# A step of its own for the layer norm's factor in the projection stage of a windowed-attention layer

## The chip, the core and the metric

The kernel runs on one core of one Trainium2 chip. The metric is the device time of one execution in microseconds (us), the median of several runs. The engines are TensorE (PE in the profile, PEld for its weight loads), VectorE (DVE), ScalarE (ACT), GpSimd (POOL) and SyncE (SP), which issues the transfers.

## The reference, cut to what matters

One transformer layer on x of shape 4 x 2048 x 256: x + attention(norm(x)), then a feed-forward part with ternary weights on the norm of that. The change lies in the first norm, ahead of the projections:

```python
def _layernorm(x, axis=-1, eps=1e-05):
    m = jnp.mean(x, axis=axis, keepdims=True)
    v = jnp.var(x, axis=axis, keepdims=True)
    return (x - m) / jnp.sqrt(v + eps)
...
        q = (x @ Wq.T).reshape(Bb, Tt, H, HD).transpose(0, 2, 1, 3)
        k = (x @ Wk.T).reshape(Bb, Tt, H, HD).transpose(0, 2, 1, 3)
        v = (x @ Wv.T).reshape(Bb, Tt, H, HD).transpose(0, 2, 1, 3)
```

Here x is already the normed one. Attention has 16 heads of 16, a window of 128 keys on either side, and key 0 visible to all. All is float32.

## The kernel before, in words

The kernel has a projection stage (`stage_project`, about 0 to 218 us), then one block with attention and the feed-forward part. Only the projection stage is touched in substance.

**Tiling.** The 8192 rows of x are 16 groups g of 512 rows, each group 4 blocks (t) of 128 rows. A group passes through a software pipeline of steps. In step i an engine works on different groups at once: `at(lag)` is group i - lag. Before the change the lags are LN = 1 (statistics and factor), LT = 2 (turning, that is transposing the normed rows), LP = 3 (projection). x itself is loaded by SP in step i = g (L337).

**The norm of a group.** VectorE: four `bn_stats` (L137), four `bn_aggr` that give mean and variance (L145), variance + eps (L148). ScalarE: the square root (L152). VectorE again, in `rstd`: reciprocal r0 (L158) and one Newton step in four small operations, t = (v+eps)*r0 (L160), t = t*r0 (L162), t = 1.5 - 0.5t (L164), rstd = t*r0 (L166); then `shifts`, shift = -mean*rstd (L195). All of these work on tiles of 128x4, and each waits for the one before it. In the next step ScalarE writes xn = x*rstd + shift, one 128x256 block at a time (L201, `scale_act`), TensorE turns the eight 128x128 pieces into two PSUM banks (L444, `turn()`), ScalarE copies them out as xt_hi (L569) and VectorE subtracts to get xt_lo (L673).

**The projection of a group q.** TensorE makes four banks u = 0 to 3 (two of Q, two of K) with `three_pass` (L221 to L223, 6 matmuls of 512 columns for each bank), with `turn()` of the next group between u = 2 and u = 3, then four blocks of V (24 matmuls of 272 columns). For each u: ScalarE copies the high bf16 part (`high`, L537), VectorE the rest (`rest_of`, L651 for Q, L655 for K), ScalarE the middle part (`mid`, L542), GpSimd the low part (L394, a 128x512 subtraction of two SBUF tiles), and for K a small fill of a gap column (L405, at the start of a sequence also L403). ScalarE copies V out (`v`, L547). SP stores the parts (L345, L351), V (L353), and then loads the next x (L337); SP does all of this in the order of the code.

**The order inside a step is written out by hand for each engine.** ScalarE before: xn 0 and 1, high(0), xn 2, high(1), xn 3, high(2), xt_hi twice, mid(0), high(3), v(0), mid(1), v(1), root, mid(2), v(2), mid(3), v(3). VectorE before: rest(0), stats 0 and 1, rest(1), stats 2, rest(2), xt_lo twice, stats 3, rest(3), `spread` (aggregate and eps), `rstd`, `shifts`, then the weights' parts (`dve_part`: sums of absolute values L910, and in eleven of the steps, two more operations each on 128x256, L931 and L933).

**The start.** Steps 0 to 2 are run by hand among the preparations: VectorE handles group 0, then the x0 row, `w_low(0)`, the statistics of group 1, q0, step LT, `w_low(1)`, wv_lo, and then the steps from LP on. GpSimd copies wv_hi for the other sequences there (L384).

`weights`, `Group`, `wait`, `step` are as in the listing; `wait` is a semaphore wait that is left out for a value of zero.

## Time and profile before

| | us |
|---|---|
| median of 3 runs | 1227.88 |
| lowest and highest run | 1227.07, 1853.66 |
| the profiled execution, its own time | 1227.89 |
| its span in the profile | 1226.1 |
| PE busy | 1156.5 |
| DVE busy | 1017.4 |
| ACT busy | 826.1 |
| POOL busy | 696.1 |

The profiled execution's own time is 1.8 us over its span, and equals the median. In the timeline rows below the columns are start (us), duration (us), engine, line, operation, written tile <- read tiles, shapes and count; in brackets stands the idle time of the engine before it and what ended that. Successive operations of one engine overlap a little in their records, so the distance from start to start is what an operation costs in a row of them. The projection stage's steady steps lie between 30 and 185 us. The granted clock of TensorE was full there (1.00).

### The profile page before, as it was taken

What the parts mean: (1) busy time and instruction counts of PE and PEld (TensorE: products, weight loads), DVE (VectorE), ACT (ScalarE), POOL (GpSimd) and SP (SyncE); (2) the same over time, 40 slices, a digit from 0 to 9 for tenths busy, and PEclk for the clock granted to TensorE, in tenths of its full rate; (3) what the DMA queues carried; (4) which work ended last, traced back from release to release, by engine and by line L of the source; (5) the groups of instructions that cost most, each with busy time, mean ns of one, the idle gap of its engine ahead of it and who ended that gap; (6) DMA issues with size and microseconds to landing.
All of it is one profiled execution on the core that took longest, in us unless ns stands there. A gap on an engine that the chain in (4) does not pass through costs nothing.

```text
span 1226.1 us, 26405 instructions
## 1 busy us (share of the span) xinstructions
PE 1156.5 (94%) x9051; PEld 762.1 (62%) x9051; DVE 1017.4 (83%) x3202; ACT 826.1 (67%) x1381; POOL 696.1 (57%) x930
## 2 busy tenths in 40 slices
PE   6888888599999999999999999999999999999997
PEld 5777775144444444444444444445889889889886
DVE  6889984788888888888888888886788888888885
ACT  5777774067777877777777777776665565565564
POOL 4445443457777777777777777676443343343344
PEclk8999998589999999999999999999999999999999
DMA  4797863854345643565435654314031221221200
GB/s 142 236 285 240 253 215 132 153 131 108 103 113 131 150 118 89 123 153 120 122 103 125 146 131 106 102 39 155 20 102 53 71 85 52 71 85 53 70 18 35
DMA packets 141253, 145.23 MB, mean 118 GB/s; under 512 B 23084, under 2 KB 134720, under 8 KB 141120
## 3 DMA queue, kind: packets, MB, share of 16 engines
q1 hardware_dynamic: 141120, 143.55, 44.0%
q8 instruction: 72, 1.18, 0.4%
q14 instruction: 61, 0.50, 0.2%
HBM read 91.74 MB, written 50.95 MB: 116 GB/s over the span
## 4 chain that ended last, share of the span: by engine, by line
PE 64%; DVE 7%; SPq 5%; issue 2%; DMA 1%; POOL 1%; ACT 1%; DVEq 0%; POOLq 0%
PE e_psum L1361 14%; PE e_psum L1403 13%; PE e_psum L1381 12%; PE e_psum L1671 5%; PE e_psum L1673 5%; SPq L1191 4%; PE e_psum L1651 3%; PE e_psum L1652 3%; PE e_psum L1099 2%; DVE n_stats L137 2%; DVE f_x L1770 2%; DMA e_q<-a_shift 1%; PE e_psum L1656 1%; PE e_psum L1620 1%; PE e_psum L223 1%
## 5 line engine op out<-in xcount | busy, mean ns | idle before, releaser
L1499 DVE CUSTOM_DVE_ANT_0 a_masked<-e_psum,a_band 128x387 f32<-128x387 f32 (+1 forms) x1024 | 502.7, 536 | 74.3 <-PE e_psum L1361 68.3
L1455 ACT ACTIVATE a_weights<-e_psum 128x1024 f32<-128x1024 f32 x384 | 385.8, 1022 | 111.2 <-PE e_psum L1381 111.1
L1361 PE MATMUL e_psum<-e_k,e_q 96*128 96x387 bf16 (+1 forms) x1024 | 328.0, 332 | 15.2 <-DMA e_q<-q_parts 11.2
L1260 POOL TENSOR_SCALAR_AFFINE_SELECT a_weights<-a_weights 128x1024 f32<-128x1024 f32 x256 | 275.7, 1090 | 51.4 <-ACT a_weights L1455 51.4
L1381 PE MATMUL e_psum<-e_q,e_k 128*128 128x384 bf16 (+2 forms) x1408 | 271.6, 278 | 6.9 <-DMA e_q<-a_shift 5.9
L1712 POOL TENSOR_TENSOR f_square<-f_relu 128x512 f32<-128x512 f32 x128 | 144.3, 1128 | 210.6 <-ACT f_relu L1701 198.9
L1361 PEld LDWEIGHTS e_psum<-e_k,e_q 96*128 96x128 bf16 x1024 | 93.8, 97 | 203.6 <-DVE a_max L1499 104.2
L1403 PE MATMUL e_psum<-a_weights,a_v 128*17 128x384 f32 (+2 forms) x2816 | 208.0, 393 | 1.3 <-POOL a_weights L1260 1.1
L1381 PEld LDWEIGHTS e_psum<-e_q,e_k 128*128 128x128 bf16 x1408 | 136.8, 99 | 65.1 <-DMA e_q<-a_shift 7.6
L1671 PE MATMUL e_psum<-w_w_t,f_square_hi 128*128 128x256 f32 x512 | 129.0, 287 | 5.5 <-DVE f_square_lo L1758 5.5
L1673 PE MATMUL e_psum<-w_w_t,f_square_lo 128*128 128x256 f32 x512 | 125.9, 281 | 0.0
L1701 ACT ACTIVATE f_relu<-e_psum,w_mag 128x512 f32<-128x512 f32 x128 | 87.5, 684 | 52.5 <-PE e_psum L1656 52.5
L1758 DVE TENSOR_TENSOR f_square_lo<-f_square,f_square_hi 128x512 fp32r<-128x512 f32 x128 | 98.6, 791 | 24.1 <-POOL f_square L1712 24.1
L1671 PEld LDWEIGHTS e_psum<-w_w_t,f_square_hi 128*128 128x128 f32 x512 | 96.2, 188 | 15.2 <-DVE f_square_lo L1758 12.0
L1651 PE MATMUL e_psum<-f_xt_hi,w_w_t 128*128 128x512 f32 x256 | 102.8, 402 | 1.1 <-ACT f_relu L1701 1.1
L1652 PE MATMUL e_psum<-f_xt_lo,w_w_t 128*128 128x512 f32 x256 | 101.2, 395 | 0.0
L1673 PEld LDWEIGHTS e_psum<-w_w_t,f_square_lo 128*128 128x128 f32 x512 | 96.5, 188 | 2.9
L1403 PEld LDWEIGHTS e_psum<-a_weights,a_v 128*17 128x17 f32 x2816 | 55.2, 96 | 65.6 <-issue 61.3
L394 POOL TENSOR_TENSOR p_q_parts<-p_rest,p_q_parts 128x512 bf16<-128x512 f32 x32 | 38.0, 1188 | 88.3 <-ACT p_q_parts L542 88.3
L1268 POOL TENSOR_TENSOR a_shift<-a_neg_rest,a_shift 16x128 bf16<-16x128 f32 x64 | 26.7, 417 | 107.4 <-ACT a_shift L1461 107.4
L1704 ACT ACTIVATE f_square_hi<-f_relu 128x512 fp32r<-128x512 f32 x128 | 81.0, 633 | 4.1
L1499 DVE DVE_READ_ACCUMULATOR2_ANT a_max<- 128x1 f32 x1024 | 83.6, 82 | 0.0
(207 smaller groups left out, 2046.3 us busy)
## 6 DMA issues: line engine op xcount, KB each, us to landing
k_parts<-p_k_parts SPq DMA_DIRECT2D x96, 129.0 KB, 2.8
e_k<-k_parts SPq DMA_DIRECT2D x64, 193.5 KB, 3.8
e_k<-k_parts SPq DMA_DIRECT2D x192, 64.5 KB, 3.3
q_parts<-p_q_parts SPq DMA_DIRECT2D x96, 128.0 KB, 3.0
e_q<-q_parts SPq DMA_DIRECT2D x64, 192.0 KB, 3.5
e_q<-q_parts SPq DMA_DIRECT2D x192, 64.0 KB, 3.2
v_ones<-p_va SPq DMA_DIRECT2D x16, 544.0 KB, 3.7
p_x<-in_x SPq DMA_DIRECT2D x16, 512.0 KB, 5.6
```

Source lines behind the costliest of these rows:

```text
L1260: pool.affine_select(out=blocks, in_=blocks, compare_op=ALU.is_ge, fill=0.0, base=0, pattern=[[0, NQ // 2 * HEAD_COLS // P // CUT_STEP], [ ...
L1361: pe.matmul(turn[TURN_OF_TILE[j] % TURN_BANKS][:, lo:hi], qw[ux.q][0:SLOT_ROWS, h, t * P:t * P + P], kt[ux.hq][0:SLOT_ROWS, h, start + lo: ...
L1381: ins = pe.matmul(score[c % 2][:, (n % 2) * GT + col * P:(n % 2) * GT + (col + m) * P], kt[us.hq][:, h, k0:k0 + P], qw[us.q][:, h, qb * P: ...
L1403: ins = pe.matmul(sum_bank[32 * j:32 * j + VW, qb * P:(qb + m) * P], vw[:, up.gpar, kb + 1, h * VW:h * VW + VW], pe_w[:, up.upar, c0:c0 + ...
L1455: act.activation(pe_w[:, us.upar, c * CHUNK:(c + 1) * CHUNK], score[c % 2][:], ACT.Exp).then_inc(s_exp, 1)
L1499: dve.tensor_tensor_reduce(out=masked[:, ux.upar, h, t:t + hi - lo], in0=bank[:, lo:hi], in1=band[:, lo:hi], scale=1.0, scalar=NEG, op0=AL ...
L1651: pe.matmul(self.h_bank[j % 2][:], lhs, self.sh.xt_hi[:, q.par, k, :], start=(k == 0), stop=False)
L1652: pe.matmul(self.h_bank[j % 2][:], lhs, self.sh.xt_lo[:, q.par, k, :], start=False, stop=False)
L1671: pe.matmul(y, sh.r2_hi[:, j % 4, part], self.w.w2_t[:, j, :], start=(j == 0 and t == 0), stop=False, skip_group_check=True)
L1673: ins = pe.matmul(y, sh.r2_lo[:, j % 4, part], self.w.w2_t[:, j, :], start=False, stop=(j == MH - 1), skip_group_check=True)
L1712: pool.tensor_tensor(sh.r2[:, j % 4, :], sh.r[:, j % 4, :], sh.r[:, j % 4, :], ALU.mult).then_inc(self.s_sq, 1)
L1758: dve.tensor_tensor(sh.r2_lo[:, j % 4, :], sh.r2[:, j % 4, :], sh.r2_hi[:, j % 4, :].bitcast(F32), ALU.subtract).then_inc(self.s_r2lo, 1)
```

## The change

The norm's factor (root, reciprocal, Newton step, shift) leaves the step of the statistics and gets a lag of its own, LF = 2; turning moves to LT = 3 and projection to LP = 4. ScalarE's root now adds eps itself through its bias, reads the variance tile, and stands between high(0) and xn 2 in place of between v(1) and mid(2). VectorE's separate eps addition goes; the Newton step is two `scalar_tensor_tensor` after the first product in place of three operations: t = (v + eps)*r0, t = (-0.5 t)*r0, rstd = (t + 1.5)*r0. The reciprocal and the first product stand after rest(0) and stats 0, the others after rest(1). The statistics are spread otherwise: block 0 after rest(0), block 1 after xt_lo, blocks 2 and 3 with the aggregate after rest(3). The statistics of group 2 are taken by hand before the first projection step. Cut to its core:

```diff
+        self.eps = sb("eps", [P, 1])
...
     def blocks(self, v, x, q, blocks):
+        if 0 in blocks:
+            wait(v, self.s_step, q.g * 3)
...
+    def aggregate(self, v, q):
+        v.wait_ge(self.s_step, q.g * 3 + 1)
+        for t in range(TB):
+            ins = v.bn_aggr(self.mv[:, q.par, t, :], self.stats[:, t, :])
+        ins.then_inc(self.s_step, 2)
+
+    def root_eps(self, a, q):
+        a.wait_ge(self.s_step, q.g * 3 + 3)
+        a.activation(self.sd[:, q.par, :], self.mv[:, q.par, :, 1], ACT.Sqrt, bias=self.eps[:, 0:1]
+                     ).then_inc(self.s_sd, 1)
+
+    def factor_begin(self, v, q):
+        base = q.g * 3
+        v.wait_ge(self.s_sd, q.g + 1)
+        v.reciprocal(self.r0[:], self.sd[:, q.par, :]).then_inc(self.s_back, 1)
+        v.wait_ge(self.s_back, base + 1)
+        v.scalar_tensor_tensor(out=self.t0[:], in0=self.mv[:, q.par, :, 1], scalar=EPS, in1=self.r0[:],
+                               op0=ALU.add, op1=ALU.mult).then_inc(self.s_back, 1)
+
+    def factor_end(self, v, q):
+        base = q.g * 3
+        v.wait_ge(self.s_back, base + 2)
+        v.scalar_tensor_tensor(out=self.t0[:], in0=self.t0[:], scalar=-0.5, in1=self.r0[:],
+                               op0=ALU.mult, op1=ALU.mult).then_inc(self.s_back, 1)
+        v.wait_ge(self.s_back, base + 3)
+        v.scalar_tensor_tensor(out=self.rs[:, q.par], in0=self.t0[:], scalar=1.5, in1=self.r0[:],
+                               op0=ALU.add, op1=ALU.mult).then_inc(self.s_shift, 1)
+        v.wait_ge(self.s_shift, q.g * 2 + 1)
         v.scalar_tensor_tensor(out=self.shift[:, q.par], in0=self.mv[:, q.par, :, 0], scalar=-1.0,
                                in1=self.rs[:, q.par], op0=ALU.mult, op1=ALU.mult).then_inc(self.s_shift, 1)
...
-        LN, LT, LP = 1, 2, 3
+        LN, LF, LT, LP = 1, 2, 3, 4
...
                     high(0)
+                if f:
+                    norm.root_eps(act, f)
                 if t:
                     norm.scale_act(act, xb[:, t.ring], xn[:, t.par], t, (2,))
...
                     v(1)
-                if n:
-                    norm.root(act, n)
-                if q:
                     mid(2)
...
-                first = n if n and n.g != 1 else None
+                first = n if n and n.g not in (1, 2) else None
...
                     rest_of(0)
                 if first:
                     dve.wait_ge(s_x[n.ring], (n.turn + 1) * DMA)
-                    norm.blocks(dve, xb[:, n.ring], n, (0, 1))
+                    norm.blocks(dve, xb[:, n.ring], n, (0,))
+                if f:
+                    norm.factor_begin(dve, f)
                 if q:
                     rest_of(1)
-                if first:
-                    norm.blocks(dve, xb[:, n.ring], n, (2,))
+                if f:
+                    norm.factor_end(dve, f)
                 if q:
                     rest_of(2)
...
                 if first:
-                    norm.blocks(dve, xb[:, n.ring], n, (3,))
+                    norm.blocks(dve, xb[:, n.ring], n, (1,))
                 if q:
                     rest_of(3)
                 if first:
-                    norm.spread(dve, n)
-                if n:
-                    norm.rstd(dve, n)
-                    norm.shifts(dve, n)
+                    norm.blocks(dve, xb[:, n.ring], n, (2, 3))
+                    norm.aggregate(dve, n)
...
             dve.wait_ge(s_x[1], DMA)
-            norm.front(dve, xb[:, 1], Group(1))
+            norm.blocks(dve, xb[:, 1], Group(1), range(TB))
+            norm.aggregate(dve, Group(1))
...
                               wv_hi[:, :, :, D:D + H].bitcast(F32), ALU.subtract).then_inc(s_clo, 1)
+            dve.wait_ge(s_x[2], DMA)
+            norm.blocks(dve, xb[:, 2], Group(2), range(TB))
+            norm.aggregate(dve, Group(2))
             for i in range(LP, G + LP):
```

The feed-forward part's norm still uses `front`, `root` and `rstd`; it gets the one added wait of `blocks`.

## Rows read from the trace of the kernel before

**Rows 1.** Busy time of each engine in two projection steps; columns named in the first line.

```profile
core 0: us, PE busy (x) PEld busy (x) DVE busy (x) ACT busy (x) POOL busy (x), PEclk, DMA share, GB/s
...
85.50:96.80 11.30, 9.74 (x58) 8.33 (x57) 9.81 (x24) 8.63 (x20) 4.97 (x7) 1.00 0.93 292
96.80:108.10 11.30, 9.74 (x58) 8.31 (x57) 10.76 (x25) 8.63 (x20) 4.97 (x7) 1.00 0.77 247
```

**Rows 2.** Waits of 40 to 180 us: us in total, times, longest us.

```profile
ACT p_xn L201 <- DVE n_shift L195: 23.4, 13, 2.0
```

**Rows 3.** Timeline of PE, one step.

```profile
102.44 1.09 PE L444 MATMUL p_bank<-p_ident,p_xn 128*128 128x128 f32 x8 [1.56 <-ACT p_xn L201]
...
107.84 0.40 PE L221 MATMUL p_bank<-p_xt_hi,p_wt_hi 128*128 128x512 f32 x1
...
111.80 0.40 PE L223 MATMUL p_bank<-p_xt_hi,p_wt_lo 128*128 128x512 f32 x1
```

**Rows 4.** Timeline of ACT, the end of one step and the start of the next.

```profile
108.24 0.39 ACT L547 ACTIVATE p_va<-p_bank 128x272 f32<-128x272 f32 x1
110.67 1.09 ACT L201 ACTIVATE p_xn<-p_x,n_shift,n_rstd 128x256 f32<-128x256 f32 x2 [2.04 <-DVE n_shift L195]
```

**Rows 5.** Timeline of DVE, the norm's factor in one step.

```profile
106.61 0.17 DVE L148 TENSOR_SCALAR n_var_eps<-n_meanvar 128x4 f32<-128x4 f32 x1
107.05 0.18 DVE L158 RECIPROCAL n_rstd_first<-n_stddev 128x4 f32<-128x4 f32 x1 [0.27 <-ACT n_stddev L152]
107.26 0.65 DVE L160 TENSOR_TENSOR n_newton<-n_var_eps,n_rstd_first 128x4 f32<-128x4 f32 x1
107.94 1.05 DVE L162 TENSOR_TENSOR n_newton<-n_newton,n_rstd_first 128x4 f32<-128x4 f32 x1
...
109.23 1.14 DVE L166 TENSOR_TENSOR n_rstd<-n_newton,n_rstd_first 128x4 f32<-128x4 f32 x1
110.41 0.16 DVE L195 SCALAR_TENSOR_TENSOR n_shift<-n_meanvar,n_rstd 128x4 f32<-128x4 f32 x1
110.49 0.43 DVE L931 TENSOR_TENSOR z_below<-z_w_in,z_nhalf 128x256 f32<-128x256 f32 x1
```

**Rows 6.** Timeline of POOL at the same time.

```profile
107.84 1.13 POOL L394 TENSOR_TENSOR p_k_parts<-p_rest,p_k_parts 128x512 bf16<-128x512 f32 x1
...
109.23 1.13 POOL L394 TENSOR_TENSOR p_k_parts<-p_rest,p_k_parts 128x512 bf16<-128x512 f32 x1
110.44 0.25 POOL L405 TENSOR_TENSOR p_k_parts<-p_key,p_one 128x12 bf16<-128x12 bf16 x1
```

**Rows 7.** Timeline of ACT, then of PE: turns of the first, second and last step.

```profile
24.55 0.59 ACT L201 ACTIVATE p_xn<-p_x,n_shift,n_rstd 128x256 f32<-128x256 f32 x1
...
25.26 1.03 PE L444 MATMUL p_bank<-p_ident,p_xn 128*128 128x128 f32 x8
...
35.60 1.09 PE L444 MATMUL p_bank<-p_ident,p_xn 128*128 128x128 f32 x8 [0.58 <-ACT p_xn L201]
...
179.67 1.09 PE L444 MATMUL p_bank<-p_ident,p_xn 128*128 128x128 f32 x8 [1.56 <-ACT p_xn L201]
```

**Rows 8.** Timeline of ACT, DVE and PE before the first projection step.

```profile
13.21 2.08 ACT L201 ACTIVATE p_xn<-p_x,n_shift,n_rstd 128x256 f32<-128x256 f32 x4 [2.05 <-DVE n_shift L195]
...
15.63 0.38 DVE L145 BATCH_NORM_AGGREGATE n_meanvar<-n_stats 128x2 f32<-128x6 f32 x4
...
15.34 1.97 PE L444 MATMUL p_bank<-p_ident,p_xn 128*128 128x128 f32 x8 [0.25 <-ACT p_xn L201]
```

**Rows 9.** Timeline of DVE, then of POOL: both busy on SBUF tiles.

```profile
166.52 0.48 DVE L933 SCALAR_TENSOR_TENSOR z_w_in<-z_w_in,z_half,z_below 128x256 f32<-128x256 f32 x1
...
166.62 0.49 POOL L405 TENSOR_TENSOR p_k_parts<-p_key,p_one 128x12 bf16<-128x12 bf16 x1
```

**Rows 10.** The load of x: timeline of SP, then landing times of all tile loads.

```profile
102.44 0.57 SPq L337 DMA_DIRECT2D p_x<-in_x  x1
...
DMA to landing us min/median/max: 5.0/5.6/10.8
```

More of the change, by code:

```diff
@@ L190, in rstd_power @@
         ins.then_inc(self.s_back, 5)
-    def shifts(self, v, q):
-        v.wait_ge(self.s_back, q.g * 5 + 5)
+    def aggregate(self, v, q):
[23 more added lines that the diff above has]
+        v.wait_ge(self.s_shift, q.g * 2 + 1)
         v.scalar_tensor_tensor(out=self.shift[:, q.par], in0=self.mv[:, q.par, :, 0], scalar=-1.0,
@@ L198, in scale_act @@
     def scale_act(self, a, x, xn, q, blocks):
-        a.wait_ge(self.s_shift, q.g + 1)
+        a.wait_ge(self.s_shift, q.g * 2 + 2)
         for t in blocks:
@@ L530, in body @@
             def body(at):
-                q, t, n = at(LP), at(LT), at(LN)
+                q, t, f = at(LP), at(LT), at(LF)
                 def high(u):
@@ L614, in _ @@
             dve.memset(ones[:], 1.0)
+            dve.memset(norm.eps[:], EPS)
             dve.wait_ge(s_x0, DMA)
@@ L642, in body @@
             def body(at):
-                q, t, n = at(LP), at(LT), at(LN)
-                first = n if n and n.g != 1 else None
+                q, t, f, n = at(LP), at(LT), at(LF), at(LN)
+                first = n if n and n.g not in (1, 2) else None
                 def rest_of(u):
```

## The prediction
> **What bounds the kernel now.** I read the busy time by stretches first. In a projection step of 11.3 us every engine has room: PE 9.74, ACT 8.63, DVE 9.8 to 10.8, POOL 4.97, the transfers a share of 0.77 to 0.93 [rows 1]. No engine is full, so a loop of waits sets the step. The waits of the stage name it: ScalarE stands 23.4 us in 13 steps before its first xn, for the shift of VectorE [rows 2]. The timelines show the loop. ScalarE is done with its last V copy by 108.6, and starts xn at 110.67, 2.04 us later, right behind the shift of 110.41 [rows 4, 5]. TensorE reaches `turn()` and idles for xn 3, 1.56 us by its record [rows 3]. Then all that follows in the step (xt_hi, xt_lo, the rests, statistics, aggregate, factor, shift) is late by as much. So the factor at the end of a VectorE step is on the path, since the next step begins with its use.
>
> Why is that factor so long? From the eps addition to the end of the shift's slot VectorE needs 106.61 to 110.49 = 3.88 us [rows 5] for operations on 4 elements per partition. The reciprocal costs 0.21 from start to start, the shift 0.16 us, but the three products take 0.65, 1.05 and 1.14. The first ends at 107.91 and the second at 108.99, as GpSimd's operation on two SBUF tiles ends at 108.97; the third spans 109.23 to 110.37, GpSimd's next one 109.23 to 110.36 [rows 5, 6]. The small products wait for GpSimd's big ones to finish. Some 2.3 of the 3.88 us are such waits.
>
> **The change part by part.** *TensorE's floor for a step.* From `turn()` at 102.44 to bank 0 of the next group at 107.84 it is 5.40 us with no idle time; the 18 matmuls of u = 0 to 2 begin at 107.84 and the last at 111.80, spaced (111.80 - 107.84)/17 = 0.233, so 4.19. Together 9.59 us [rows 3]. Turns of the second and the last step lie 179.67 - 35.60 = 144.07 us apart for 13 steps, 11.08 each [rows 7]. From the start of group 1's projection (25.26 + 5.40 = 30.66) to that of group 15 (179.67 + 5.40 = 185.07) it is 154.4 us for 14 steps. At the floor they take 14 x 9.59 = 134.3. So 20.1 us is all that there is to win in these steps.
>
> *The factor a step earlier.* The shift of the group that is to be turned is now ready most of a step before ScalarE wants it, so both that 2.04 and the 1.56 go. What is late next? I walk a step of 9.6 from T, the start of bank 0. ScalarE's last V copy started 0.40 after T (108.24 against 107.84) and moves up by the root's 0.1 that has gone from ahead of it; xn 0 and 1 start near T+0.6 and end T+1.6, when bank 0 is complete (six matmuls at 0.233 and 0.2 for the result). High(0), the root and xn 2 end before bank 1 at T+3.0; high(1) (about 0.5) and xn 3 (0.59, rows 7) end at T+4.1. `turn()` is due at T+4.19. That fits by less than 0.1 us. The first step of the trace shows that it does fit: xn 3 runs 24.55 to 25.14, the turn starts at 25.26 with no idle time in its record [rows 7]. ScalarE's 8.63 a step lie under 9.6. I take 9.6.
>
> *VectorE.* Removed are busy times of 0.17 + 0.18 + 0.65 + 1.05 + 0.17 (the constant step, taken as the other small ones) + 1.14 + 0.16 = 3.52 and 0.27 of waiting for the root [rows 5]. Added are five small ones, reciprocal, three products and the shift, at 0.17 each (no row shows the fused product at this size except the shift, 0.16; ends 0.16, and 1.14 if GpSimd is in the way) = 0.9. Its heaviest step falls from 10.76 to 8.1, a common one from 9.81 to 7.2 [rows 1]. But the waits move: L931, which started at 110.49, when GpSimd had only its 0.25 us fill left, now starts near T+9.1, in the middle of GpSimd's burst. L931 and L933 can wait up to 1.1 together or each (half and half, 1.1 taken). That makes 8.3 to 9.2, under 9.6; its cover is that rest(0) of the next step is not needed by mid(0) until T+5.9.
>
> *Root, bias, wait.* The root is one operation of the same size, 0.1 us of ScalarE in a gap ahead of bank 1: nothing. If that gap is gone, 14 x 0.1 = 1.4. The wait ahead of stats 0 and the memset of eps: nothing, at most 0.05 x 32 steps of both norms = 1.6, below nothing no row gives a reason.
>
> *The place in the step.* GpSimd's burst ends at 110.69, 2.85 after T [rows 3, 6]; in the new cadence at 2.8 to 3.3, since L931 and L933 now push in. The first product stands behind rest(0) and stats 0: bank 0 at 1.6, two passes of about 0.6 (estimate, by the 0.59 of rows 7), stats 0.4, reciprocal 0.2, so near T+3.4. It just misses the burst. That a fused product also takes part in the conflict is in the trace: L933, of that kind and with two SBUF tiles, runs 166.52 to 167.00, and GpSimd's fill of 166.62 takes 0.49 in place of 0.25 [rows 6, 9]. The Trainium skill says as much (SBUF — State Buffer, section "SBUF: two separate sides": GpSimd and a VectorE operation with two SBUF inputs exclude one another for the whole instruction, first come first served). By that rule turning the products into another opcode frees nothing, only their number and place do; the second rival is that case.
>
> *SP and the x load.* SP's order stays, 13 stores and then x. x was issued at 102.44, 5.9 after its step's T (107.84 - 11.3 = 96.5), and lands 5.6 later [rows 10], so at T+11.5 to 12, which at 9.6 is 1.9 to 2.4 into the next step. Stats 0 want it at about 2.8. Before there were some 5 us of room, now 0.5. A late x first eats VectorE's slack (xt_lo of the next group is complete near T+6.8 and due at T+9.6), so up to 2.8 more is free. The transfers themselves need 0.77 x 11.3 = 8.7 us a step, in three steps around a large weights load 0.93 x 11.3 = 10.5 [rows 1]; those lag by 0.9 each, 2.7 in all, about the slack. I add 1 us, between 0 and 2.7.
>
> *The start.* Here the change loses. Before, xn 0 to 3 of group 0 ran 13.21 to 15.29 and the turn began at 15.34. Now the root of group 1 stands between xn 1 and xn 2 in ScalarE's queue, and waits for the aggregate of group 1, which ends at 16.01 [rows 8]. Then root, xn 2 and 3 (0.1 + 0.6 + 0.6 with hops): the turn begins at 17.3, 1.95 later, and the first projection step shifts by that. Bounds 0.5 and 2.5: group 0's last product starts within 0.1 us of a long GpSimd copy, and if it gets ahead VectorE is 1.5 earlier. The statistics of group 2 by hand lie beside the first bank of matmuls, nothing. One step more in the pipeline costs nothing else: x of all first groups is loaded anyway, and the last step is as before.
>
> *Sum.* 1227.89 - 20.1 + 1.95 + 1 = 1210.7. The profiled run's 1227.89 equals the median, so no scaling.
>
> **The rivals.** *1. ScalarE feeds the turn too late.* The margin is under 0.1 us. For: it also waits on high(1), which can't start before bank 1. Against: the first step. If each turn slips 0.5, 14 x 0.5 = 7: 1217.7.
>
> *2. The port conflict only moves.* Factor products and L931/L933 meet GpSimd in every step, two waits of 1.1 more: 8.1 to 9.2 becomes some 10.3, VectorE sets the step, 14 x 0.7 = 10: 1220.7. For: 0.1 us of distance to the burst. Against: only in half of the steps does L931 run, and a wait of factor_begin is followed by a full idle stretch of GpSimd.
>
> *3. Slower, through the x load.* One loop: x lands, stats 0, first half of the factor, rest(1), rest(2), xt_lo, rest(3), mid(3), GpSimd's low part and fill, four last stores, the issue of the x after next. It goes round in two steps. Behind stats 0 I count some 9.1 us, with 5.6 of landing 14.7, so 7.4 a step: not the limit. The loop allows a step of (9.1 + landing)/2. It decides above a landing of 2 x 9.6 - 9.1 = 10.1 us; the kernel is slower than before when a step passes 11.03 - 1.95/14 = 10.9, that is from a landing of 12.7. The longest landing was 10.8, with four loads queued [rows 10]. At 14.5 a step is 11.8: 1227.9 + 14 x 0.77 + 1.95 = 1240.6. Speaking for it: transfers at 0.77 x 11.3/9.6 = 0.91 of their time.
>
> *4. The change does nothing to the loop* (something else holds ScalarE at the step's head): 1227.9 + 1.95 = 1229.8. Against it stands only one name in the waits.
>
> **How the numbers follow.** Forecast 0.72, rival 1 0.12, rival 2 0.10, rival 3 0.02, rival 4 0.02, 0.02 for a gain beyond TensorE's idle time. The time is the forecast's, 1210.7. The range goes from 1207.0 (all 20.1, the start at 0.5, nothing added) to 1218.5, which takes in rival 1 and stops short of rival 2. Over 2% is 24.6 us, about what a measurement of this kernel can tell from no change. The forecast's 17 are 1.4%, and even 20.1 would be within 2%: faster 0.02 (the gain beyond TensorE's idle time), slower 0.01 (half of rival 3, with landings above 16 us), within 2% 0.97.
>
> **What would show it.** In the profile after: turns 9.6 to 9.7 apart between the second and the last step; TensorE without idle time before them; ScalarE's first xn no longer waiting for L195's successor; small products of 0.17 in steady steps; L931 at 0.4 to 1.5 near the end of the step; the first turn at 17.3; stats 0 waiting for x in few steps or none. Wrong if the turns are 10.3 apart or more, if TensorE still idles before L444, if stats 0 wait for the x load in most steps, or if the stage gains as said and the time doesn't, the attention block giving it back.

## The result, and the profile after

The changed kernel took 1212.09 us (median of 4 runs, 1211.71 to 1213.96), the kernel before 1228.36 (median of 4 runs: three of 1227.07 to 1228.83, and a slow one of 1853.66 that the ratio leaves out). The ratio is 0.9874 [0.9855, 0.9893]: 1.3% faster, less than 2%. Forecast were 1210.7 us, in a range of 1207.0 to 1218.5. The profiled execution took 1211.89 us with a span of 1210.1, so 16.0 us less than the profiled one before.

The waits of the projection stage that bear on the change come first, between 30 and 170 us of the kernel after (engine, line, tile <- what it waited for: us in total, times, longest):

```profile
...
DVE n_stats L140 <- DMA p_x<-in_x: 10.7, 7, 3.1
...
PE p_bank L475 <- ACT p_xn L231: 1.6, 3, 0.5
```

ScalarE's wait for the shift, 23.4 us in 13 steps [rows 2], is gone. TensorE waits before three turns in place of every one. In its place stands a new name: VectorE waits for the x load in 7 steps, up to 3.1 us.

The busy time of a free step and of one with a late x, which answers to [rows 1] (stretch, length, busy us and instructions of PE, PEld, DVE, ACT, POOL, granted clock, DMA share, GB/s):

```profile
60.80:70.40 9.60, 9.60 (x59) 8.39 (x58) 9.31 (x26) 8.86 (x20) 5.20 (x8) 1.00 1.03 330
119.40:130.20 10.80, 10.46 (x61) 8.91 (x60) 8.47 (x23) 8.77 (x19) 6.34 (x9) 1.00 0.85 267
```

In the free step TensorE is full. The transfers there have a share of 1.03, around a weights load, and yet the step isn't longer.

VectorE's timeline of one step after (start, us, engine, line, operation), which answers to [rows 5]:

```profile
94.38 0.15 DVE L211 RECIPROCAL n_rstd_first<-n_stddev 128x4 f32<-128x4 f32 x1
94.57 0.16 DVE L213 SCALAR_TENSOR_TENSOR n_newton<-n_meanvar,n_rstd_first 128x4 f32<-128x4 f32 x1
...
95.26 0.15 DVE L219 SCALAR_TENSOR_TENSOR n_newton<-n_newton,n_rstd_first 128x4 f32<-128x4 f32 x1
95.44 0.16 DVE L222 SCALAR_TENSOR_TENSOR n_rstd<-n_newton,n_rstd_first 128x4 f32<-128x4 f32 x1
95.64 0.16 DVE L225 SCALAR_TENSOR_TENSOR n_shift<-n_meanvar,n_rstd 128x4 f32<-128x4 f32 x1
...
99.77 0.89 DVE L966 TENSOR_TENSOR z_below<-z_w_in,z_nhalf 128x256 f32<-128x256 f32 x1
100.69 1.23 DVE L968 SCALAR_TENSOR_TENSOR z_w_in<-z_w_in,z_half,z_below 128x256 f32<-128x256 f32 x1
```

GpSimd beside it, which answers to [rows 6]:

```profile
93.64 0.26 POOL L436 TENSOR_TENSOR p_k_parts<-p_key,p_one 128x12 bf16<-128x12 bf16 x1
97.36 1.17 POOL L425 TENSOR_TENSOR p_q_parts<-p_rest,p_q_parts 128x512 bf16<-128x512 f32 x1 [3.46 <-ACT p_q_parts L573]
```

GpSimd's burst (its run of low parts and fills) ends at 93.90, the first product begins at 94.57, and GpSimd begins again only at 97.36. Every product takes 0.15 to 0.16 us, where the three of before took 0.65, 1.05 and 1.14. Of the 39 products between 30 and 175 us 36 are as short; the other three are the second product (L219) at 77.61, 126.62 and 146.74, with 0.53, 0.54 and 0.79 us. These are the three steps in which x comes latest (below), so that the factor slides into GpSimd's next operation. The price moved to the weights' operations: here L966 and L968 take 0.89 and 1.23; over ten steps their medians are 0.97 and 0.49, where before they were 0.44 and 0.49.

ScalarE at the head of the next step, which answers to [rows 4]: the last V copy, xn 0 and 1, high(0), the root, xn 2, high(1) and xn 3 follow each other with no bracket of idle time:

```profile
100.62 0.41 ACT L578 ACTIVATE p_va<-p_bank 128x272 f32<-128x272 f32 x1
100.90 1.10 ACT L231 ACTIVATE p_xn<-p_x,n_shift,n_rstd 128x256 f32<-128x256 f32 x2
...
102.42 0.29 ACT L205 ACTIVATE n_stddev<-n_meanvar,n_eps 128x4 f32<-128x4 f32 x1
...
103.82 0.59 ACT L231 ACTIVATE p_xn<-p_x,n_shift,n_rstd 128x256 f32<-128x256 f32 x1
```

TensorE's turns after, which answer to [rows 3, 7]: the first, the second, two of the three that are late, and the last:

```profile
17.69 1.97 PE L475 MATMUL p_bank<-p_ident,p_xn 128*128 128x128 f32 x8 [2.69 <-ACT p_xn L231]
26.86 1.04 PE L475 MATMUL p_bank<-p_ident,p_xn 128*128 128x128 f32 x8
...
85.38 1.09 PE L475 MATMUL p_bank<-p_ident,p_xn 128*128 128x128 f32 x8 [0.53 <-ACT p_xn L231]
...
134.39 1.09 PE L475 MATMUL p_bank<-p_ident,p_xn 128*128 128x128 f32 x8 [0.52 <-ACT p_xn L231]
...
164.36 1.03 PE L475 MATMUL p_bank<-p_ident,p_xn 128*128 128x128 f32 x8
```

From 26.86 to 164.36 it is 137.50 us for 14 steps, 9.82 each. Eleven of the distances are 9.51 to 9.60, three are 10.81 to 10.83 (ending at 85.38, 134.39 and 154.77). Some 9 us ahead of each of the three VectorE's first statistics wait for x:

```profile
76.39 0.43 DVE L140 BATCH_NORM_STATS2 n_stats<-p_x 128x6 f32<-128x256 f32 x1 [3.11 <-DMA p_x<-in_x]
...
```

At 125.39 and 145.51 the same wait is 2.15 and 2.81. The other four, of 0.43 to 0.95 us, delay no turn. From issue to landing all x loads together still take a median 5.6 us [rows 10], and those of the steady steps, 35 to 155 us, are these:

```profile
DMA to landing us min/median/max: 5.2/5.3/7.5
```

The median hides something. The three loads behind the three late turns, issued at 68.88, 118.71 and 138.53, landed after 7.5, 6.7 and 7.0 us; the other eight after 5.2 to 5.8. Had they landed after 5.3, VectorE would by my estimate have waited 0.9, 0.75 and 1.1 us for them; waits up to 0.95 here and up to 1.41 in e8 delay no turn. So behind each late turn stand two things, a load issued late in its step and a load that lands slowly.

Why is it issued late? SP, which had waits of its own before, has almost none now:

```profile
88.70 0.57 SPq L368 DMA_DIRECT2D p_x<-in_x  x1
...
93.73 4.93 SPq L382 DMA_DIRECT2D k_parts<-p_k_parts  x6
98.71 0.59 SPq L384 DMA_DIRECT2D v_ones<-p_va  x1
99.35 0.56 SPq L368 DMA_DIRECT2D p_x<-in_x  x1
99.95 4.40 SPq L376 DMA_DIRECT2D q_parts<-p_q_parts  x6
104.39 3.84 SPq L382 DMA_DIRECT2D k_parts<-p_k_parts  x6
```

(SPq is SP issuing transfers; x6 are six issues in a row.) 0.56 + 4.40 + 3.84 + 0.59 and the 0.04 us between them make a round of 9.56 us; where an issue is dearer, as among the K stores of 93.73 (one of them takes 1.68), it is 10.65. Record by record, between 45 and 155 us, SP's 155 issues after take 102.7 us with one gap above 0.2 us in all, of 0.45. The 144 of before take 93.1, with 18 gaps above 0.2 that sum to 11.7. So SP became full with the new step. x goes out once in a round, and its place in the step slides: relative to its step's T (4.19 before the turn) it is issued at 6.2 in the second step, 8.05 in the fifth, 9.5 in the eleventh. Of the 1.85 us between the second and the fifth, 1.19 are one more issue on SP, the large weights load at 58.76.

The sum of the profiled runs:

| | predicted | measured |
|---|---|---|
| start, to the turn of the first projection step | +1.95 | +1.60 (26.86 - 25.26) |
| 14 steps at TensorE's floor | -20.1 | -21.0 (14 x 9.53 against 154.4) |
| late x | +1 | +4.1 (137.50 - 133.4) |
| last turn to the end | 0 | -0.7 |
| all | -17.2 | -16.0 |

VectorE's first masking of scores in the attention block comes at 214.13 after and 229.96 before, 15.8 earlier; from there to the end it is 996.0 and 996.1 of the spans. So the attention block gives nothing back.

### The profile page after: what moved, and what is told of

The parts are those of the page before. It is cut to its first block, busy times and chain, and to the rows that moved or that the text cites. A ratio compares the mean times of both kernels' runs of the same rounds, so it can differ in the third digit from the quotient of the medians.

```text
span 1210.1 us, 26404 instructions
## 1 busy us (share of the span) xinstructions
PE 1153.2 (95%) x9051; PEld 761.2 (63%) x9051; DVE 992.7 (82%) x3171; ACT 828.2 (68%) x1381; POOL 699.3 (58%) x930
## 4 chain that ended last, share of the span: by engine, by line
PE 64%; SPq 7%; DVE 6%; issue 3%; DMA 1%; POOL 1%; ACT 1%; DVEq 0%; POOLq 0%
PE e_psum L1396 14%; PE e_psum L1438 13%; PE e_psum L1416 11%; PE e_psum L1706 5%; PE e_psum L1708 5%; SPq L1226 4%; PE e_psum L1686 3%; PE e_psum L1687 3%; PE e_psum L1134 2%; DVE n_stats L140 2%; DVE f_x L1805 2%; DMA e_q<-a_shift 1%; SPq L1224 1%; PE e_psum L1691 1%; PE e_psum L251 1%
## 5 line engine op out<-in xcount | busy, mean ns | idle before, releaser
L1686 PE MATMUL e_psum<-f_xt_hi,w_w_t 128*128 128x512 f32 x256 | 102.7, 401 | 1.1 <-ACT f_relu L1736 1.1
```

The source lines that it names most:

```text
L1686: pe.matmul(self.h_bank[j % 2][:], lhs, self.sh.xt_hi[:, q.par, k, :], start=(k == 0), stop=False)
```

## Experiments

Each ratio is to the kernel before. Between the lowest and the highest run of one kernel lie 2 to 7 us, part of it from the attention block (from the stage's end to the end of the program the profiles of e0 to e3 take 995.2 to 998.7), so beside the time I give the start of that block in the profiled run ("stage end": 229.96 before, 214.13 after). It is of one run only, which in e1 and e2 was the slowest. What each edit is compared with is the changed kernel, unless said otherwise.

**e0: the changed kernel again**, as the partner for e1 to e3.

> The changed kernel itself, as the measure for the three beside it: 1212 us, turns 9.53 us apart where VectorE doesn't wait for x, three gaps of 10.8, the first turn near 17.7 us.

Measured: 1210.26 us (1209.22 to 1212.86), ratio 0.9867 [0.9852, 0.9882], stage end 212.92. VectorE waits for x in 7 steps again, 9.6 us in all. The late turns are at 84.69 and 134.32, the same steps as the first two of the changed kernel's three, and again the loads behind them landed slowly, after 6.7 and 7.3 us (the others after 5.3 to 5.9). e1, e4 and e7 are late in these two steps as well, so it isn't chance which step is late.

**e1: the root of group 1 behind xn 3 at the start.**

```diff
-                if f:
+                if f and (q or not t):
                     norm.root_eps(act, f)
...
                     norm.scale_act(act, xb[:, t.ring], xn[:, t.par], t, (3,))
+                if f and t and not q:
+                    norm.root_eps(act, f)
```

> Only the start: in the one step that turns group 0, the root of group 1 stands behind xn 3 and not between xn 1 and xn 2. Theory (the change loses about 2 us there, since xn 2 waits behind that root for the aggregate of group 1): the first turn begins near 15.9 in place of 17.69, everything behind it is as much earlier, 1212.1 - 1.8 = 1210.3 us. Rival (something else, the w_low copies or the load of x, is as late): the first projection matmul moves by under 0.5 us and so does the time.

Measured: the first turn at 15.19 in place of 17.21, 2.0 earlier. But 1210.6 us (1209.83 to 1212.65), ratio 0.9869 [0.9855, 0.9882], stage end 214.83. VectorE's waits for x grew to 12.6 us. Where did the 2.0 go? By the next turn 1.27 are left, because TensorE's half clock lasts longer into an earlier step (see the last section). Those 1.3 us last until the turn of 133.01 (134.32 in e0). Behind it e1 has two more late turns, at 143.50 and 154.35, and ends 0.97 behind e0; at 120.0 one Q store took SP 2.73 us to issue, the dearest issue in the steady steps of any run, and the next load of x went out 11.72 us after the last. So the profile shows the gain kept through twelve turns and lost to an event that no other run has, in the slowest of the four runs. Neither it nor the medians tell what the start is worth by itself.

**e2: x of a group issued a step earlier.** This takes the late x away, whether the issue or the landing made it late; it doesn't tell these two apart.

```diff
-                if q := at(0):
+                if q := at(-1):
                     wait(sp, norm.s_scaled, q.g - 4 + 1)
                     sp.dma_start(xb[:, q.ring], ...)
+                if q := at(0):
                     weights.load(sp, q.g)
...
+            sp.dma_start(xb[:, 0], ...).then_inc(s_x[0], DMA)
             sweep(body, LP)
```

> Each x is loaded one step earlier (SP issues group i + 1 in step i), nothing else. Theory (the x load lands too late in the shorter steps, and that is what is left above TensorE's floor): no wait of VectorE for x, all 13 turn distances 9.53 us, so 13 x (9.84 - 9.53) = 4.0 us less, 1208.1 us. Rival (the 16 DMA engines are the bound, share above 0.9): the lateness goes to the stores or stays with x, the turns stay at 9.8 on average, 1211 to 1212 us.

Measured: no wait for x; the turns 9.50 to 9.54 apart but for the first distance (9.64) and two near the end (9.74 and 10.20), the last at 160.95, 2.0 earlier than in e0. The time is 1209.59 us (1207.82 to 1212.29), ratio 0.986 [0.9843, 0.9877], stage end 211.82. The stage shows the gain, the time alone doesn't tell it from scatter. What is late next are K stores, near the end; whether by their issue or by their landing I didn't look:

```profile
ACT p_k_parts L570 <- DMA k_parts<-p_k_parts: 3.2, 3, 1.5
```

ScalarE waits to overwrite a K tile until its store of two steps ago has landed.

**e3: both edits.**

> The two edits together: if they are independent, 1212.1 - 1.8 - 4.0 = 1206.3 us, TensorE without a gap of over 0.3 us between the first and the last projection step. If the two have a common cause (transfers), less than 4 us in all, 1208 us or more.

Measured: 1206.46 us (1205.21 to 1207.96), ratio 0.9837 [0.9823, 0.985], stage end 207.36. The turns run from 24.04 to 157.44 and are all 9.49 to 9.54 apart but for the first distance of 9.60 (one turn's record is missing; the two steps around it take 19.05). TensorE's busy time in the windows of e3, and of the changed kernel, each from 26 us on, to behind its last turn:

```profile
26.00:160.00 134.00, 134.00 (x790) 117.03 (x789) 113.89 (x291) 122.69 (x267) 73.76 (x92) 1.00 0.86 266
```

```profile
26.00:166.00 140.00, 137.41 (x801) 118.75 (x800) 112.84 (x295) 125.07 (x270) 73.80 (x92) 1.00 0.82 257
```

TensorE has no idle time left. The edit of the start, which showed no gain in e1, goes with 3.1 us less than e2; in the profiles the second turn is 2.6 earlier than in e2. That the start's gain needs the room which the earlier x makes is argued, not shown: e1 lost it to one dear issue, and with 4 or 5 runs each the medians can't settle a difference of 2 to 3 us.

**e4: the old arithmetic at the new places.** The lags, the places and the spread of the statistics stay; eps is added on VectorE, and the Newton step has its four operations.

```diff
+        v.tensor_scalar(self.ve[:, q.par, :], self.mv[:, q.par, :, 1], EPS, None, ALU.add)
...
-        v.scalar_tensor_tensor(out=self.t0[:], in0=self.mv[:, q.par, :, 1], scalar=EPS, in1=self.r0[:], ...)
+        v.tensor_tensor(self.t0[:], self.ve[:, q.par, :], self.r0[:], ALU.mult)
...
-        v.scalar_tensor_tensor(out=self.t0[:], in0=self.t0[:], scalar=-0.5, in1=self.r0[:], ...)
-        v.scalar_tensor_tensor(out=self.rs[:, q.par], in0=self.t0[:], scalar=1.5, in1=self.r0[:], ...)
+        v.tensor_tensor(self.t0[:], self.t0[:], self.r0[:], ALU.mult)
+        v.tensor_scalar(self.t0[:], self.t0[:], -0.5, 1.5, ALU.mult, ALU.add)
+        v.tensor_tensor(self.rs[:, q.par], self.t0[:], self.r0[:], ALU.mult)
```

> The changed kernel's lags and places with the old arithmetic (eps by an operation of its own, Newton step in four operations, tensor_tensor products). Theory (the lag did it, the arithmetic lies in VectorE's slack): VectorE 0.4 to 0.6 us more a step, a step stays at TensorE's 9.53, only the three steps in which x is late may lose some 0.4 more each: 1212 to 1213.5 us. Rival (the saved operations matter): 1216 us or more.

Measured: 1211.76 us (1209.76 to 1216.51), against 1227.2 before: 0.988 [0.9865, 0.9896], stage end 213.82. The products by their tile (count; min/median/max ns, first and last start):

```profile
L214 DVE TENSOR_TENSOR n_newton<-n_var_eps,n_rstd_first x16: 161/161/164, 10.5 to 153.4; 128x4 f32<-128x4 f32 x16
L219 DVE TENSOR_TENSOR n_newton<-n_newton,n_rstd_first x16: 150/152/1136, 10.7 to 154.1; 128x4 f32<-128x4 f32 x16
```

At this place the old products are as short as the new ones (the two long ones, 0.73 and 1.14, are again in the late steps). With its place given, the fewer operations are worth nothing that shows.

**e5: the new arithmetic at the old place.** Lags, places and statistics as before; only the fused operations and the root with its bias are new.

```diff
-        LN, LF, LT, LP = 1, 2, 3, 4
+        LN, LT, LP = 1, 2, 3
...
                     v(1)
+                if n:
+                    norm.root_eps(act, n)
...
                     norm.aggregate(dve, n)
+                if n:
+                    norm.factor_begin(dve, n)
+                    norm.factor_end(dve, n)
```

> The kernel before with nothing but the new arithmetic: lags, and the factor at the end of VectorE's step, in GpSimd's burst, as before. Theory (a fused product with two SBUF inputs waits for GpSimd as a plain one does): the products still take 0.5 to 1.1 us where GpSimd subtracts, the step falls by 0.2 to 1.0 us from 11.08: 1214 to 1225 us, 1220 taken. Rival (the fused form doesn't take part in the conflict): all products at 0.16, the step falls by 3.0 us at once, to TensorE's 9.6: 1208 us.

Measured: 1215.86 us (1214.42 to 1219.34), ratio 0.9913 [0.9901, 0.9926], stage end 216.92; the turns mostly 10.12 apart, 10.21 on the mean. That is 11.3 us of the gain, for the arithmetic alone. The three products in VectorE's timeline of a common step, and GpSimd's operations beside them:

```profile
120.87 0.55 DVE L215 SCALAR_TENSOR_TENSOR n_newton<-n_meanvar,n_rstd_first 128x4 f32<-128x4 f32 x1
121.46 1.04 DVE L221 SCALAR_TENSOR_TENSOR n_newton<-n_newton,n_rstd_first 128x4 f32<-128x4 f32 x1
122.53 0.16 DVE L224 SCALAR_TENSOR_TENSOR n_rstd<-n_newton,n_rstd_first 128x4 f32<-128x4 f32 x1
```

```profile
121.36 1.12 POOL L426 TENSOR_TENSOR p_k_parts<-p_rest,p_k_parts 128x512 bf16<-128x512 f32 x1
122.56 0.25 POOL L437 TENSOR_TENSOR p_k_parts<-p_key,p_one 128x12 bf16<-128x12 bf16 x1
```

The first product waits for the GpSimd operation before these rows, the second for the one that started at 121.36. The third begins at 122.53, just before GpSimd's next operation at 122.56, and takes 0.16 us. Before, a `tensor_scalar` of 0.17 us stood between the second and the third product, so that the third began together with GpSimd's next large subtraction (109.23 and 109.23 in rows 5 and 6) and took 1.14. In three of the steps, with first products at 90.66, 100.87 and 111.08, it goes the other way round: two products take 0.16 each and the third meets GpSimd for 1.11 us. So a fused product takes part in the conflict like the others, as the prediction had it; the arithmetic gains because, with one operation fewer ahead of the third product, one long wait for GpSimd in each step falls away. The Trainium skill (SBUF — State Buffer, section "SBUF: two separate sides") calls it an exclusive lock for the whole instruction that goes to whichever of the two starts first; these rows agree, 121.36 against 121.46 and 1.04 us for a product of 0.16.

**e6: the own lag without the place.** As the changed kernel, but the factor stands at the end of VectorE's step, behind the aggregate.

```diff
-                if f:
-                    norm.factor_begin(dve, f)
                 if q:
                     rest_of(1)
-                if f:
-                    norm.factor_end(dve, f)
...
                     norm.aggregate(dve, n)
+                if f:
+                    norm.factor_begin(dve, f)
+                    norm.factor_end(dve, f)
```

> The changed kernel with the factor moved, within its own lag, from the head of VectorE's step to its end behind the aggregate, in GpSimd's burst. Theory (the place matters by the port conflict, but little since the result isn't needed until the next step): products of up to 1.1 us again, VectorE 1.5 to 2.3 us more a step, 8.7 to 10.4 in all, so only the steps with the weights' operations pass 9.53: 1213 to 1220 us, 1216 taken. Rival (only the lag matters): 1212 us. Second rival (the place is what the change is about): steps of 10.4 throughout, 1224 us.

Measured: 1220.72 us (1218.08 to 1221.17), ratio 0.9942 [0.993, 0.9954], stage end 222.15. The turns are 10.30 to 10.32 apart between 27.77 and 161.82 (the last distance is 9.75). The wait of before is back, though shorter (23.4 us in 13 steps then [rows 2]):

```profile
ACT p_xn L231 <- DVE n_shift L225: 12.8, 14, 0.9
```

and the products meet GpSimd, the first for 0.44 us and the second for 1.06:

```profile
105.47 1.06 DVE L219 SCALAR_TENSOR_TENSOR n_newton<-n_newton,n_rstd_first 128x4 f32<-128x4 f32 x1
```

The lag by itself buys only that the root is ready; a factor at the end of a step is used at the head of the next, whichever group it is of. The time lies above my range of 1213 to 1220, and the steps are those of the second rival (10.4 throughout). e6 is also 4.9 us slower than e5, which has no lag of its own: e6 keeps the changed kernel's spread of the statistics, two blocks and the aggregate right ahead of the factor. No run separates that spread from the lag and the place.

**e7: one small load more on SP** (64 bytes, ahead of each V store), the first test of SP's round.

```diff
+                    wait(sp, s_idle, DMA * q.g)
+                    sp.dma_start(idle_row[:], x[0:1, 0:1, 0:16].rearrange("b a d -> (b a) d")).then_inc(s_idle, DMA)
```

> The changed kernel with one more transfer issued by SP in each projection step, 64 bytes into an unused tile. Theory (SP's own issuing is what is full: in the changed kernel its 14 issues follow one another with 0.04 us between them, some 9.6 us a step): the issue adds 0.45 to 0.65 us to SP's round, which can't hide, the x loads go out later and later, the turns fall to 9.53 + 0.5 on average, 13 x 0.5 = 6 to 8 us more: 1216 to 1219 us. Rival (the 16 DMA engines are full, or the landing alone is late): 64 bytes are nothing, 1210 to 1212 us.

Measured: 1212.83 us (1209.88 to 1216.24), ratio 0.9879 [0.9859, 0.9899], stage end 214.18. That misses my range of 1216 to 1219. But it tells nothing apart, because the round hardly grew: the load took 0.45 us to issue, and the two issues behind it became cheaper (V 0.38 in place of 0.59, x 0.50 in place of 0.56). Rounds without a dear issue went from 9.54 to 9.62 us to 9.77 to 9.82, and the mean of ten rounds from 10.01 to 10.10. (The expectation of e10 below still has 0.12 for the growth.)

**e8: V stored from GpSimd**, behind its last fill. SP has 13 issues a round.

```diff
-                    sp.wait_ge(s_vout, q.g * TB + TB)
-                    sp.dma_start(va_dram[...], va[...]).then_inc(s_vstored, DMA)
...
+                    pool.wait_ge(s_vout, q.g * TB + TB)
+                    pool.dma_start(va_dram[...], va[...]).then_inc(s_vstored, DMA)
```

> The changed kernel with the V store issued by GpSimd behind its last fill and not by SP; same bytes, 13 issues on SP. Theory (SP's issuing is full): SP's round falls by 0.6 us to 9.0, under TensorE's 9.53, x goes out at the same place of each step, the waits for x and the three gaps of 1.3 us go: 4 us less, 1206 to 1208 us. Rival (the DMA engines are full): no change, 1210 to 1212 us. Against both: GpSimd's time for issuing, up to 1 us a step beside 5.2 of work, and its effect on VectorE are not in any trace so far; if they matter, 1213 us or more.

Measured: 1208.94 us (1207.67 to 1212.12), ratio 0.985 [0.983, 0.9869], stage end 211.01. All turns from 36.76 to 160.51 are 9.49 to 9.54 apart; VectorE waits for x 5.0 us in 6 steps, at most 1.41, and no turn is late. The time is 0.9 above my range of 1206 to 1208, and its interval overlaps that of e0, so it is the turns that show the effect. But SP is still nearly full: its round is 9.6 us from 68.91 to 136.09 (9.95 in the changed kernel), since one K store in nearly each now takes 1.2 to 1.5 us to issue, in the stretch in which GpSimd issues V (0.77 us of GpSimd):

```profile
98.01 0.59 SPq L368 DMA_DIRECT2D p_x<-in_x  x1
98.65 3.86 SPq L376 DMA_DIRECT2D q_parts<-p_q_parts  x6
102.55 4.76 SPq L382 DMA_DIRECT2D k_parts<-p_k_parts  x6
```

Whether one store delays the other, or these dear issues come from something else, I didn't try. And the loads land sooner as well, after 5.0 to 6.0 us. The load behind the changed kernel's first late turn shows what that does. It goes out at 68.91 here and at 68.88 there, but lands after 6.0 us in place of 7.5, VectorE waits 1.41 in place of 3.11, and the turn that follows comes on time:

```profile
74.97 0.43 DVE L140 BATCH_NORM_STATS2 n_stats<-p_x 128x6 f32<-128x256 f32 x1 [1.41 <-DMA p_x<-in_x]
```

So e8 doesn't show that the issuing alone made x late. The Trainium skill (DMA: Bandwidth & Descriptors, section "Rules for kernel authors") says that spreading transfers over issuing engines doesn't help bandwidth and only saves the sequencer's issue time; here the 0.6 us taken off SP's round came back in part, and the round fell by 0.35.

**e9: e3 and e8 together.**

> The root behind xn 3 at the start, x a step earlier, and the V store on GpSimd together. Turns at 9.53 throughout were already had with the first two (1206.5 us), so by either theory there is nothing left in the projection steps: 1205.5 to 1207 us.

Measured: 1205.45 us (1204.99 to 1207.85), ratio 0.9823 [0.9806, 0.984], stage end 207.80. As fast as e3 within the scatter: with TensorE full already, nothing is left for it to win. By its median it is the fastest version that ran, with e3 beside it as the simpler one.

**e10: two 128-row loads more on SP** ahead of the K stores, 64 bytes a row. e7 had been too light; this one should lengthen the round by over 1 us and adds 16 KB to the some 2.6 MB that a step moves.

```diff
+                    wait(sp, s_idle, 2 * DMA * q.g)
+                    for n in range(2):
+                        sp.dma_start(idle_rows[:, n], x[0, n * P:(n + 1) * P, 0:16]).then_inc(s_idle, DMA)
```

> The changed kernel with two more loads issued by SP in each projection step ahead of the K stores, 128 rows of 64 bytes each, 16 KB in all beside 2.6 MB. The single 64-byte transfer before cost 0.45 us and made the two issues behind it 0.27 us cheaper, so it lengthened SP's round by 0.12 us only. Theory (SP's issuing is full): two issues of 128 rows lengthen it by 0.8 to 1.2 us, from 9.85 to 10.6 to 11.0, the turns follow at 10.4 or more: 13 x 0.6 = 8 us and up, 1217 to 1224 us. Rival (the transfers are full or late, not their issue): 0.6% more bytes, 1210 to 1213 us.

Measured: 1224.42 us (10 runs, 1221.28 to 1226.46), against 1227.64 before: 0.9973 [0.9963, 0.9983], stage end 225.70. That is all but 3 us of the gain lost to two issues a step. SP's timeline of two rounds, and the waits of e10:

```profile
84.67 0.57 SPq L369 DMA_DIRECT2D p_x<-in_x  x1
...
89.72 1.06 SPq L381 DMA_DIRECT2D p_idle_rows<-in_x  x2
...
95.25 0.56 SPq L369 DMA_DIRECT2D p_x<-in_x  x1
...
107.01 0.57 SPq L369 DMA_DIRECT2D p_x<-in_x  x1
```

```profile
DVE n_stats L140 <- DMA p_x<-in_x: 23.4, 11, 4.5
```

The two rounds take 10.58 and 11.76 us, the ten rounds from 39.27 to 150.35 11.11 on the mean, 1.1 more than in the changed kernel (10.01), which is what the two issues cost; the nine distances between turns from 64.76 on average 11.18. From 35 to 155 us x lands after 5.2 to 6.2 us, median 5.3. And over the same stretch the transfers move less than in the changed kernel:

```profile
35.00:155.00 120.00, 110.98 (x626) 93.08 (x626) 91.95 (x242) 98.92 (x212) 57.25 (x72) 1.00 0.82 248
```

```profile
35.00:155.00 120.00, 117.41 (x681) 101.18 (x681) 101.34 (x268) 107.05 (x232) 63.66 (x81) 1.00 0.88 274
```

(e10 first, the changed kernel second; DMA share and GB/s are the last two numbers.) A bound by transfers would show a higher share, a bound by landing a longer one. Neither is there, and the step follows SP's round. So SP's issuing by itself can make x late and set the step, here with no slow landing at all. For the changed kernel it shows one of the two parts; what the three slow landings of 6.7 to 7.5 us add to the slide is not measured, since no run changes the landing alone.

## Why the prediction was right, and which step failed

- *What bounds the kernel* held: with the wait for the shift gone, the turns came from 11.03 to 9.82 apart, and in e3 to 9.53.
- *TensorE's floor* was 9.53, not 9.59. The forecast took it from turns that had idled; a turn that follows without idle time takes 1.04 us in place of 1.09. Worth 0.9 us over 14 steps.
- *The factor a step earlier*: ScalarE's margin of under 0.1 us was enough. In a step without a late x TensorE shows no idle time. Rival 1 fell.
- *VectorE and the place*: products of 0.15 to 0.16, L966 at 0.89, as said. The distance from GpSimd's burst was wider than thought, 0.67 us in place of 0.1, and rival 2 fell, but for 0.4 to 0.6 us in the three late steps. e4, e5 and e6 show what the edits are worth: place and lag alone (with the new spread of the statistics) 15.4 us, arithmetic alone 11.3, both 16.4, the lag and the arithmetic without the place 6.5. The two overlap: each takes the same wait away.
- *The fused product in the conflict*: shown by e5, and at the start, where L222 at 11.81 takes 1.47 us beside a GpSimd copy that began at 11.79:

```profile
11.79 1.47 POOL L415 CAST p_wv_hi<-p_wv_hi 128x1536 fp32r<-128x1536 f32 x1 [2.73 <-ACT p_wv_hi L619]
11.81 1.47 DVE L222 SCALAR_TENSOR_TENSOR n_rstd<-n_newton,n_rstd_first 128x4 f32<-128x4 f32 x1
```

- *The start*: the first turn at 17.69 (17.3 forecast), 2.35 later than before, of which 0.39 is an x load that landed later. By the next turn 1.60 is left (below). Whether the program gets this back when it is taken away is open (e1, e3).
- ***SP and the x load* is the step that failed**, though the total hid it. I took +1 us, at most 2.7, and it was 4.1 in the profiled run. The sign and the place were right, the reason was wrong for the greater part. I sized it by transfers (0.77 x 11.3 = 8.7 us a step) and by the landing of 5.6, and wrote that x goes out 5.9 after T, as before. It doesn't: that was a time at which SP still had to wait for its data. Its 14 issues take 9.56 us at the least, 0.03 above TensorE's floor, and 0.3 to 1.2 us above it in a round with a dear issue or with the weights load. So in a step of 9.53 SP can't keep the place, and x slides back in the step, from 6.2 to 8.05 and 9.5 after T. The second part is landing, which I took at 5.6: it was 7.5, 6.7 and 7.0 us for the three loads behind the three late turns. Around the first of them the transfers had a share of 1.11, so the lag behind the weights load that I had reckoned with is perhaps in it; around the other two it was 0.95 and 0.97, as around loads that landed in 5.2 and 5.3. In seven steps the two came out even: SP's rounds from 68.88 to 138.53 are 9.95 each, the distances of turns from 65.02 to 134.39 9.91. e10 shows the first part, with the round 1.1 us longer and no slow landing. e2 and e8 take the late x away, but give room to both parts.
- *The signs that I had named* were in part against me: the turns are 9.82 apart and not 9.6 to 9.7, and the first statistics wait for x in 7 of the 13 steps that take them, "most steps" by my own words.
- *The range*: its lower end doesn't follow from its terms. 1227.89 - 20.1 + 0.5 is 1208.3, not 1207.0.
- Rival 3 had the late x, but by a loop that counts only the last four of SP's stores and the load's own issue; that loop allows 7.4 us a step and never bound. It left out that all 14 issues have to fit in a step. Rival 4 fell with the first view.

The two errors on the other side (floor 0.9, start and end 1.1) made up for two thirds of the 3.1 us. That the total came within 1.2 us in the profiled runs (-17.2 against -16.0) is luck by that much.

## What to carry to other kernels

When a wait that sets a loop goes, add up the round of every queue against the new step, the issuing of transfers too: a queue that waits for its data today shows free room only until you take that wait away. Small operations of one engine that have to wait for another's large ones belong where the other rests and where nobody needs them next; with that place, saving operations bought nothing that shows, without it it bought two thirds. And look at the landing of the very loads that came late, and not only at the median: here the median of 5.3 us says nothing of the three that took 6.7 to 7.5.

## What the runs showed of the hardware that was not expected

- An issue on SP has no fixed cost. In a row, a K or V store takes 0.59 to 0.61 us and 0.04 to the next, but 0.52 when SP had waited before it; the first Q store behind the x load takes 1.05, and 0.57 in e8, where no V store stands ahead of that load. Behind a 64-byte load V's issue falls to 0.38. Now and then one takes 1.3 to 1.9, once 2.73 (e1). They aren't strewn at random: the changed kernel, e0, e4 and e7 have stores that take 0.9 to 1.7 us at 53 to 55, 74 to 76, 96 to 98 and 143 to 146 us. I can't say what sets this.
- The landing of x has a pattern of its own. The load issued at 116.8 to 119.7 us lands after 6.1 to 7.3 us in the changed kernel, e0, e1, e4 and e7, where their median is 5.3 to 5.5, but after 5.1 and 5.2 in e8 and e10. Its cause is open.
- TensorE's clock. In the first projection step its granted clock is half (0.50, 1.2 GHz) at first and then full. Before, the half clock lasts from the step's start at 18.72 to about 23.6, 4.9 us; after, where the step starts at 21.07, only to about 24.4, 3.3 us. So 0.75 of the 2.35 us that the start had lost came back by the next turn, and e1 lost as much of its 2.0 us in the same way: its matmuls there are 0.43 us apart up to 23.0 us, and 0.23 behind that, while in e0, whose step starts 2.0 later, the change comes at 23.4. The windows of before and of after (the clock is the number behind POOL's):

```profile
18.70:23.60 4.90, 4.90 (x13) 3.84 (x14) 4.02 (x13) 2.46 (x5) 1.47 (x1) 0.50 0.01 2
```

```profile
21.00:24.20 3.20, 3.20 (x9) 2.54 (x9) 3.17 (x10) 1.42 (x4) 1.47 (x1) 0.50 0.51 105
...
```
